# One 4.6 MB weight load queued earlier on SyncE, and the steps of a 25-chunk recurrence spread differently between VectorE's tasks

## The reference, cut to what matters

```python
v = jnp.clip(x @ v_w + v_b, -V_MAX, V_MAX)
a = (-2.0 + v).astype(jnp.complex64) - 1j
G = bk_green_diag(a)          # d_i = a_i - 1/d_(i-1), forwards and backwards, 625 long
feats = jnp.stack([G.real, G.imag], axis=-1)
...                            # softmax gate over 8 experts, two kept: comb
h = jax.nn.gelu(jnp.einsum('bnd,edf->bnef', x, w1) + b1)
y = jnp.einsum('bnef,efd->bned', h, w2) + b2
ffn_out = jnp.einsum('bne,bned->bnd', comb, y)
spec_out = jnp.clip(feats, -10., 10.) @ out_w + out_b
return ffn_out + bk_scale * spec_out
```

## Time and profile before

| what | value |
|---|---|
| median of three runs | 1452.38 us |
| the profiled execution | 1444.31 us, its span 1442.5 us |
| PE busy | 1312.4 us (91%) |
| VectorE busy | 958.5 us (66%) |
| GpSimd busy | 647.3 us (45%) |
| ScalarE busy | 553.0 us (38%) |
| mean granted TensorE clock | 0.957 of full |

### The profile page before, as it was taken

One profiled execution on the slowest core, in us unless ns is written; L12 is line 12 of the kernel. 1 busy time (PEld: TensorE's weight loads), 2 busy tenths in 40 slices (PEclk: granted clock), 3 DMA queues, 4 the chain that ended last, 5 costly groups with the idle time before them and its releaser, 6 DMA issues.

```text
span 1442.5 us, 22867 instructions
## 1 busy us (share of the span) xinstructions
PE 1312.4 (91%) x7548; PEld 1094.2 (76%) x7548; DVE 958.5 (66%) x2154; ACT 553.0 (38%) x650; POOL 647.3 (45%) x569
## 2 busy tenths in 40 slices
PE   7988688889999969999999999999999789989991
PEld 5765588556995549999999999999767579556660
DVE  8967898877767446565666566565269875466663
ACT  0010566232420035555554545454247651223330
POOL 7025777777667544343334334433377720111103
PEclk9999898989999979999999999999999999999995
DMA  7940000020460337878778787878589752447625
GB/s 181 91 120 6 2 2 2 1 67 2 123 186 2 99 133 253 291 263 286 268 282 282 265 287 267 298 253 281 132 272 340 242 165 77 110 141 216 197 93 185
DMA packets 112660, 243.85 MB, mean 169 GB/s; under 512 B 30397, under 2 KB 52090, under 8 KB 112492
## 3 DMA queue, kind: packets, MB, share of 16 engines
q1 hardware_dynamic: 77628, 136.46, 31.6%
q0 software_dynamic: 22432, 72.27, 17.8%
q10 hardware_dynamic: 12528, 34.22, 6.1%
HBM read 202.05 MB, written 45.31 MB: 171 GB/s over the span
## 4 chain that ended last, share of the span: by engine, by line
PE 54%; POOL 18%; issue 13%; DVE 7%; DMA 6%; ACT 1%; POOLq 0%; another core or an unknown queue 0%; ACTq 0%; SPq 0%; DVEq 0%
PE PS L2707 27%; POOL evwb L795 7%; POOL zidxb L797 6%; PE PS L2910 4%; PE PS L2390 4%; PE PS L2921 3%; PE PS L2697 3%; PE PS L2836 3%; POOL edge_dram L813 2%; DMA zidxb<-zrow_dram,idxb 2%; PE PS L2878 2%; PE PS L2766 2%; DVE mlo L2148 1%; PE PS L2798 1%; DMA xg<-xn_dram,xrow 1%
## 5 line engine op out<-in xcount | busy, mean ns | idle before, releaser
L827 POOL DMA_INDIRECT xg<-xn_dram,xrow x70 | 114.9, 1641 | 281.1 <-DVEq L1527 267.8
L2707 PE MATMUL PS<-whi,xhi 128*128 128x384 f32 x840 | 221.2, 344 | 1.0 <-ACTq L1109 1.0
L2707 PE MATMUL PS<-whi,xlo 128*128 128x384 f32 x840 | 214.4, 336 | 0.0
L2707 PE MATMUL PS<-wlo,xhi 128*128 128x384 f32 x840 | 212.9, 334 | 0.0
L1318 DVE TENSOR_TENSOR wlo<-raw,whi 128x2304 fp32r<-128x2304 f32 x68 | 175.3, 2578 | 37.9 <-ACTq L1092 32.7
L1090 ACT ACTIVATE whi<-raw 128x2304 fp32r<-128x2304 f32 x68 | 145.1, 2133 | 18.8 <-DMA raw<-in_L_gnn_W_rel 9.8
L2707 PEld LDWEIGHTS PS<-wlo,xhi 128*128 128x128 f32 x840 | 152.1, 188 | 0.0
L2707 PEld LDWEIGHTS PS<-whi,xlo 128*128 128x128 f32 x840 | 151.5, 188 | 0.0
L2707 PEld LDWEIGHTS PS<-whi,xhi 128*128 128x128 f32 x840 | 148.2, 189 | 1.3 <-issue 1.3
L1318 DVE TENSOR_TENSOR xlo<-PS,xhi 128x768 fp32r<-128x768 f32 x70 | 67.0, 958 | 123.2 <-ACTq L1101 114.5
L797 POOL DMA_INDIRECT zidxb<-zrow_dram,idxb x80 | 109.4, 1367 | 31.5 <-issue 31.5
(11 more groups left out here) (452 smaller groups left out, 2590.7 us busy)
## 6 DMA issues: line engine op xcount, KB each, us to landing
raw<-in_L_gnn_W_rel SPq DMA_DIRECT2D x68, 1152.0 KB
z_dram<-xn ACTq DMA_DIRECT2D x70, 384.0 KB, 7.4
wroot<-in_L_ffn_w SPq DMA_DIRECT2D x12, 576.0 KB, 6.5
y_dram<-yb ACTq DMA_DIRECT2D x17, 384.0 KB, 3.7
pre<-in_L_ffn_w SPq DMA_DIRECT2D x9, 576.0 KB, 5.7
gw<-in_L_gnn_W SPq DMA_DIRECT2D x2, 2304.0 KB, 26.7
fw<-in_L_ffn_w SPq DMA_DIRECT2D x8, 576.0 KB
fw<-in_L_ffn_w SPq DMA_DIRECT2D x1, 4608.0 KB, 16.4
```

Source lines behind the costliest of these rows:

```text
L827: pool.indirect_dma_start(xg[b][j][:, :], None, xn_dram, bass.IndirectOffsetOnAxis(ap=xrow[:, b, j:j + 1], axis=0)).then_inc(x_gathered[b] ...
L2707: mm = pe.matmul(slot(q)[:, s * BANK:s * BANK + HALF], a[:, k, :], wt[:, k, s * HALF:(s + 1) * HALF], start=(k == 0 and part == 0), stop=( ...
```

## The change

On SP the load of fw2 moves ahead of `through_dram(2)`. On VectorE three things change. The `yield` behind the signal `spec_ready` goes, and one piece fewer is taken ahead of `chunk_low(7)`; so the signal, the wait for `spec_in` 32, the 16 copies and the first ladder step are now all one piece. That piece is taken behind `weigh_chunk(3)`. And from chunk 4 on, each `weigh_chunk` is followed by two pieces, where before that began with chunk 6. So 17 of the ladder's 24 steps stand among the chunks, where 12 did.

```diff
             load_next_pair(3)
+            sp.dma_start(fw2[:, 0:FK, :], w["L0_ffn_w2"].rearrange("e f d -> (e f) d").rearrange("(c p) d -> p c d", p=128)).then_inc(ld_f2, 16)
             through_dram(2, mat_dram, S[:, BC:BC + 2, :].rearrange("p a b -> p (a b)"),
                          ml[:, :, :], mat_dram.rearrange("(a c) m -> a c m", a=1))
-            sp.dma_start(fw2[:, 0:FK, :], w["L0_ffn_w2"].rearrange("e f d -> (e f) d").rearrange("(c p) d -> p c d", p=128)).then_inc(ld_f2, 16)
             load_comb(2)
...
                 dve.sem_inc(spec_ready, 1)
-                yield
 
                 dve.wait_ge(spec_in, 32)
...
             for c in (5, 6, 7):
-                spectral_part(8 if c < 7 else BC + 1 - 16)
+                spectral_part(8 if c < 7 else BC - 16)
                 chunk_low(c)
-            for c in range(6):
-                if c >= 4:
+            for c in range(4):
+                weigh_chunk(c)
+            spectral_part(1)
+            for c in range(4, FK):
+                if c + 4 < FK:
                     chunk_low(c + 4)
                 weigh_chunk(c)
-            for c in range(6, FK):
-                if c + 4 < FK:
-                    chunk_low(c + 4)
                 spectral_part(2)
-                weigh_chunk(c)
             for _ in spectral:
                 pass
```

## The result

| | before | after |
|---|---|---|
| median (20 runs each, in turn on the same chips) | 1451.72 us | 1463.87 us |
| lowest to highest | 1444.31 to 1457.68 | 1455.08 to 1476.25 |
| ratio after / before, 95% interval | | 1.0075 [1.0057, 1.0093] |
| the profiled execution, its span | 1444.31, 1442.5 us | 1451.72, 1449.9 us |

The change makes the kernel slower by 0.75%, which is 10.9 us of 1451.72 (the medians differ by 12.15). The time forecast was 1463.6, of an added 11.2. That these agree to 0.3 us is chance: the interval of the difference runs from 8.3 to 13.5 us.

A forecast was written before the change was run, and what follows sets the result against it. PE and GpSimd's scatters nearly tie ahead of the gather of x. 10.4 us stall + 1.5 clock - 0.7 slack = 11.2, giving 1463.6 from the median 1452.4; range 1449 to 1473 us.

The forecast's parts named there:

- The four rows it named: Profile signs: ml 10 us behind mat_dram, VectorE idle some 11, PE about 10 then half clock, gather released by x store.
- The trip: SP's DRAM write and read queue behind fw2: load through at 408.6, write 409.3, ml there at 410.9 us.
- The landing row: Profile row of fw2 landing 16.4 us after issue; not used, as its start-up is hidden by a filled queue.
- "undisturbed" trip: Write and read through DRAM without the load ahead: 4.0 us, from 399.2 to 403.2; PE then 2.7 us late.
- The chunks behind: Chunks 9 to 11: VectorE's rounds of 5.2 us against PE's 5.30, so just in time, no further PE wait.
- The clock: PE at half clock after its idle stretch ahead of chunk 8: costs 1.5 us, between 0 and 3.4.
- late and cold: Rival: fw2 takes 16.4 us from 395, ml at 413.7, PE 7 us at half speed; 15.9 us slower, 1468; chance 0.12.
- The slack of 0.7: PE side ahead of the gather of x has about 0.7 us to spare against GpSimd's scatters, subtracted from the delay.
- this stretch may fall either way: Half-speed stretch in 493 to 500, costing 3.5 us in this execution, may fall otherwise; luck of both signs.
- Cover of 11 us: GpSimd's scatters end at 522.7, the x store at about 533.9, so 11 us cover changes in GpSimd's chain.
- pass the load: Rival: the trip's 1.6 KB DMAs need not wait for fw2; X = 403.2, 2.0 us slower, 1454.4; chance 0.08.
- at no gain: VectorE's 4.56 us wait for combw of chunk 6 disappears as fw2 loads earlier, but saves no time.

The follow-up runs named there:

- half_ahead: The change with six of fw2's twelve chunks loaded ahead of the trip through DRAM and six behind, against the kernel before: ratio 1.0015 [0.9992, 1.0037].
- more_ahead: The change with load_comb(2), 0.96 MB of routing rows, also ahead of the trip in SP's queue, against the kernel before: ratio 1.0076 [1.0049, 1.0103].
- sp_undone: VectorE's part of the change alone, fw2 loaded behind the trip as before, against the kernel before: ratio 1.0052 [1.0030, 1.0073].
- early_both: The change with the yield restored, the signal ahead of chunk_low(7) and fw2 behind the trip, against the kernel before: ratio 0.9999 [0.9974, 1.0024].
- act_queue: The change with fw2 issued by ACT on its own queue instead of SP's, against the kernel before: ratio 1.0052 [1.0029, 1.0075].
- early_signal: The change with the yield restored and the signal ahead of chunk_low(7), fw2 still ahead of the trip, against the kernel before: ratio 1.0068 [1.0040, 1.0095].
- load_first: The change with fw2 loaded earlier, ahead of the third w1 pair (load_next_pair(2)), against the kernel before: ratio 1.0048 [1.0024, 1.0072].
- sp_only: SP's part of the change alone, fw2 ahead of the trip, VectorE's order as before, against the kernel before: ratio 1.0012 [0.9988, 1.0036].
- sp_only_hold: sp_only with SP holding the second relation's weight loads until three gathers of x have landed, against the kernel before: ratio 0.9980 [0.9957, 1.0003].
- spread: sp_only with the narrow spectral products of tiles 0 to 3 spread between outer's chunks of tiles 3 and 4, against the kernel before: ratio 0.9993 [0.9970, 1.0016].

## Why the prediction was right

**The mechanism.** The four rows it named are there: ml issued 10.7 us behind mat_dram, VectorE idle 12.18 us ahead of mo<-ml, PE idle 10.14 us (forecast 10.4) ahead of chunk 8 with a row at half clock behind it, and GpSimd's gather released by the x store. What makes the long trip is shown by the runs: it goes with the bytes ahead (`half_ahead`, `more_ahead`), is gone without the load (`sp_undone`, `early_both`), and is mostly the queue's order (`act_queue` against `early_signal`). Across the runs the idle time ahead of the chunks and 1.5 to 1.6 us of half clock foretell the ratio within its interval: 10.0 us for `early_signal` (measured 9.9), 5.3 for `half_ahead` (2.2, interval to 5.4), 8.8 for `act_queue` (7.6).

**The trip.** The arrival of ml was put 11.7 us behind `weigh_chunk(3)` and was 12.18. That agreement hides errors of both signs. The load was to be through 9.4 us behind the weighing and took 10.7; the write behind it was to take 0.7 and took 0.2, the read 1.6 and took 1.3. The rate was right (354 in the window above, where 346 was used). The moment from which fw2 had it to itself was not: the prediction took 395, 4.2 us ahead of the end of the weighing, and 413.0 less 4.72 MB at 354 GB/s is 399.7, 2.7 us ahead of it (an estimate from these rows). The landing row, set aside as too long, grew to 21.9 us, since it counts from an issue that now comes with other loads still ahead. PE's 10.14 us against the 10.4 forecast also hide a pair: VectorE waited 0.5 us longer, but the weighing was over 6.4 us ahead of chunk 8's due time (402.35 against 408.73), not 5.8 (399.2 against 404.96). And the 4.0 us of an "undisturbed" trip were too long: the write of the earlier trace rows stood behind the last w1 pair; in `early_both` and `load_first` it takes 1.2 us.

**The chunks behind.** Rounds of 5.2 to 5.3 us, no further wait of PE up to `outer`, no wait for combw, fw2 in time: all as forecast.

**The clock.** 1.5 forecast, 1.55 measured in the row of 3.49. The length of the idle stretch hardly mattered: the first twelve products behind 2.42, 3.78, 5.24, 7.23 and 10.14 us took 3.38, 3.47, 3.53, 3.53 and 3.49 us, and 2.04 behind 1.95 us. So 1.4 to 1.6 us is what a stall cost here, and the 7 us at half speed of *late and cold* were in no run behind a stall.

**The slack of 0.7.** This was the term that came out wrong: it was not there. The end of `outer`'s spectral products and the first relation's product with its weights, in before:

```profile
513.81 1.55 PE L2679 MATMUL PS<-fw,hT 35*125 35x384 f32 x4
...
536.66 0.99 PE L2707 MATMUL PS<-whi,xhi 128*128 128x384 f32 x2
```

From the one to the other it was 21.3 us in both executions (21.1 to 21.4 in most runs, 23.1 in `half_ahead`). The gather was indeed issued 1.3 us sooner behind `outer` (7.14 instead of 8.46), since it no longer waits for the scatters. But its first issue held GpSimd 2.52 us where it had held it 1.33, so the second came 1.2 us later behind it, and PE needs both. So the 1.3 us were lost again at once; why the issue took longer is open.

**Luck.** 10.14 + 1.55 and no slack is 11.7 us, which is what the stall costs; the narrow products gave back 1.64 us in this execution. The prediction had said that this stretch may fall either way; `outer` took 86.4, 88.0 or 89.7 us in the runs with its order unchanged.

**GpSimd.** Cover of 11 us was claimed, and 20.9 us of waiting found. The prediction allowed its chain to change by some us either way. Counted on GpSimd itself, from its copy at 395.47 us (the same in both) to the last scatter's issue, it took 118.5 us (to 514.01) instead of 124.6 (to 520.05), so 6.0 less. The gather itself came 12.5 us later (536.32 against 523.81): PE was 3.8 us later at chunk 8's due time, 10 us longer in the stage, and the issue 1.3 us sooner behind it. That the earlier end of the load is the reason for the 6.0 us is not shown. From the same copy it took 116.9 us in `sp_only` (392.35 to 509.28), but 116.9 too in `sp_undone` (397.11 to 514.05) and 124.1 in `early_both` (394.41 to 518.48), both with fw2 behind the trip. The reason stays open.

**The rivals.** The trip does not pass the load in the same queue in a way that helps: the write ended 0.2 us behind it in after and at best 0.4 us ahead (`sp_only_hold`), and `half_ahead` and `more_ahead` show it waiting for the bytes ahead. The 2.7 us of stall that the prediction gave to an undisturbed trip were 1.95 in `sp_undone`. *Late and cold* gives the write its 2.4 us in words and 0.7 in its sum; with 2.4 its time would be 1470, in the range too. The prediction had called the wait for combw gone "at no gain". Over before that is so, but with the late signal and fw2 behind the trip the same wait costs 5.24 us (`sp_undone`), which the move of fw2 saves.

## What to carry to other kernels

A small transfer that an in-order engine waits for belongs ahead of bulk loads in its queue, with the wait as late behind the signal as the work allows; on another queue it was still slowed by the traffic here (8.3 us for both directions, 2.5 with little traffic). A step moved on an in-order engine takes its place in two queues of waiting: ask what stands behind each wait now, the harmless ones of before included, and what the other engine's queue holds back until the step's signal comes (fw2 and the routing rows in `sp_undone`). Where two edits are made together, run each alone, as here a hidden stall of one half was covered by the other.

## What was not expected of the hardware

- A DMA of 1.6 KB on a queue of its own took 5.2 us to write and 3.0 us to be read back and used under 363 GB/s of other traffic (`act_queue`), and 1.2 and 1.25 us with 2 GB/s (`load_first`).
- TensorE's granted clock fell to half while PE was busy throughout, within a row of 16 products of 35 rows: 0.52 in 493 to 500 of before, which reaches into the full products behind them. With the same products in fours between full ones it stayed at 1.00 (`spread`). That the few rows are the reason was not tested apart.
- It also fell behind an idle stretch of PE of only 2.42 us: 0.50 in 393 to 395 of `load_first`.
- The same indirect gather held GpSimd for 1.33 us at 523.81 in before and for 2.52 us at 536.32 in after, and for 1.02 us at 532.33 in `sp_undone`; why is open.
